# Two further blocks per turn in the graph layers' selection loop

## The reference, cut to what matters

```
def _rgcn_conv(x, W, Wroot, b, src, dst, etype):
    xs = x[src]
    seg = dst * R + etype
    sums = jax.ops.segment_sum(xs, seg, num_segments=N * R)
    cnt = jax.ops.segment_sum(jnp.ones_like(xs[:, 0]), seg, num_segments=N * R)
    mean = sums / jnp.maximum(cnt, 1.0)[:, None]
    return x @ Wroot + b + jnp.einsum('nrd,rde->ne', mean, W)
...
h = relu(_rgcn_conv(layernorm(x), W1, ...));  x = x + _rgcn_conv(h, W2, ...)
```

## Time and profile before

| what | value |
|---|---|
| median of 3 runs | 2932.53 us (2931.82 to 2933.41) |
| profiled execution, span of its instructions | 3487.9 us |
| the two graph layers in it | about 111 to 2657 us |
| indirect gathers of both layers | 1584 x 964 ns on POOL |
| PE | busy 71% of the span, mean granted clock 0.836 |

### The profile page before, as it was taken

One profiled execution on the slowest core, in us unless ns is written; L12 is line 12 of the kernel. 1 busy time (PEld: TensorE's weight loads), 2 busy tenths in 40 slices (PEclk: granted clock), 3 DMA queues, 4 the chain that ended last, 5 costly groups with the idle time before them and its releaser, 6 DMA issues.

```text
span 3487.9 us, 82172 instructions
## 1 busy us (share of the span) xinstructions
PE 2472.0 (71%) x19212; PEld 1832.7 (53%) x19213; DVE 1780.8 (51%) x4984; ACT 1225.2 (35%) x2344; POOL 1862.5 (53%) x1980
## 2 busy tenths in 40 slices
PE   1346787678687786346776587687877428999999
PEld 0113565356365564114564365465656327888887
DVE  7324455345355454124454354354545338787777
ACT  5202343134243342012343143152432126555554
POOL 1666566655655554666556656655563543333333
PEclk9557999589799898557998798798997559999999
DMA  6223323233332232223333333333335234322222
GB/s 216 80 83 112 88 87 91 85 87 89 87 88 87 86 89 64 86 84 97 98 104 97 94 100 99 94 105 95 101 100 163 102 115 132 96 73 71 71 70 59
DMA packets 165489, 333.24 MB, mean 96 GB/s; under 512 B 36078, under 2 KB 102346, under 8 KB 165288
## 3 DMA queue, kind: packets, MB, share of 16 engines
q0 software_dynamic: 91632, 247.48, 24.1%
q1 hardware_dynamic: 39912, 41.03, 4.0%
q10 hardware_dynamic: 33872, 43.92, 3.9%
HBM read 285.39 MB, written 49.07 MB: 96 GB/s over the span
## 4 chain that ended last, share of the span: by engine, by line
PE 44%; issue 22%; DVE 10%; another core or an unknown queue 9%; DVEq 7%; SPq 2%; ACT 2%; DMA 1%; ACTq 0%; POOLq 0%; POOL 0%
PE more_banks L1408 13%; PE sum_banks L1384 9%; PE sum_banks L1385 7%; PE more_banks L1535 4%; PE sum_banks L1535 3%; PE more_banks L1400 3%; PE sum_banks L1545 3%; DVEq L1044 3%; DVEq L1041 2%; DVE sels L1044 2%; DVEq L1027 1%; DVE stage L1079 1%; DVE sels L1036 1%; PE sum_banks L1426 1%
## 5 line engine op out<-in xcount | busy, mean ns | idle before, releaser
L509 POOL DMA_INDIRECT ring<-table,tabs x1584 | 1526.9, 964 | 1046.4 <-SPq L399 670.0
L1384 PE MATMUL sum_banks<-ring,sels 128*128 x2348 | 726.6, 311 | 630.1 <-issue 420.1
L1408 PE MATMUL more_banks<-weights,stage 128*128 128x256 f16 x5292 | 919.1, 290 | 22.0 <-issue 21.4
L1385 PE MATMUL sum_banks<-ring,sels 128*128 x2348 | 732.2, 313 | 41.5 <-issue 38.7
L1384 PEld LDWEIGHTS sum_banks<-ring,sels 128*128 128x128 f16 (+1 forms) x2348 | 242.4, 103 | 928.2 <-issue 896.9
L683 ACT ACTIVATE stage<-sum_banks,inv 128x256 f16<-128x256 f32 x784 | 328.1, 473 | 789.5 <-issue 384.9
L1408 PEld LDWEIGHTS more_banks<-weights,stage 128*128 128x128 f16 x5292 | 531.1, 104 | 135.3 <-issue 37.1
L1036 DVE SCALAR_TENSOR_TENSOR sels<-lane,win_off,tabs 128x256 f16<-128x256 f16 x792 | 349.4, 482 | 422.1 <-remote 181.9
L654 ACT ACTIVATE stage<-more_banks 128x1024 f16<-128x1024 f16 x392 | 402.0, 1026 | 419.1 <-remote 405.6
L1044 DVE TENSOR_SCALAR sels<-lane,win_off,tabs 128x128 f16 x780 | 260.6, 334 | 495.8 <-issue 339.6
L1079 DVE SCALAR_TENSOR_TENSOR stage<-sum_banks,inv,stage 128x256 f16<-128x256 f32 x784 | 347.0, 479 | 57.2 <-issue 40.2
(11 more groups left out here) (319 smaller groups left out, 2407.5 us busy)
## 6 DMA issues: line engine op xcount, KB each, us to landing
ring<-table,tabs POOLq DMA_INDIRECT x1584
weights<-L_ffn_W ACTq DMA_DIRECT2D x96, 178.5 KB
stage<-L_ffn_W ACTq DMA_DIRECT2D x16, 1024.0 KB, 5.0
edge_work<-lot_in SPq DMA_DIRECT2D x54, 260.0 KB
table<-edge_work ACTq DMA_DIRECT2D x49, 128.0 KB
lot_in<-sels SPq DMA_DIRECT2D x8, 260.0 KB
weights<-L_gnn_W SPq DMA_DIRECT2D x2, 1024.0 KB, 8.3
weights<-L_gnn_W ACTq DMA_DIRECT2D x2, 1024.0 KB
```

What stands on the lines that cost most here:

```text
L509: pool.indirect_dma_start(ring_rows[:, b % RING, 0:2 * D], None, tables[layer], bass.IndirectOffsetOnAxis(row_tab[:, b:b + 1], 0)).then_in ...
L1384: pe.matmul(to[:, 0:D + 1], hot, ring_row[:, ds(at + D, D + 1)], start=first, stop=last, skip_group_check=True)
L1385: return pe.matmul(to[:, 0:D], hot, ring_row[:, ds(at, D)], start=False, stop=last, skip_group_check=True)
L1408: return [pe.matmul(ps_out[par], rows[:, xp * KD + k, :], w16[:, wp, k, r * D:(r + 1) * D], start=part == PART_ORDER[0] and n == 0, stop=p ...
```

## The change

`more_blocks` takes two blocks per turn: one `scalar_tensor_tensor` over 128x256 makes both selections, after a wait for the second of the two blocks (also where the span ends on the first, and the second belongs to the next window). It signals `more_ready` once per turn. `more_sums` on PE steps by two: one wait, the first block's `add_rows`, and under a condition the second block's. `sel_more` gets a seventeenth slot, since the second of two starts at slot 15; a constant matrix moves to another place to make room.

```diff
-        sel_more = sels[:, 4 * P:4 * P + RING * P // 2].bitcast(f16).rearrange("p (s n) -> p s n", s=RING)
+        sel_more = sels[:, 4 * P:4 * P + (RING + 1) * P // 2].bitcast(f16).rearrange("p (s n) -> p s n", s=RING + 1)
...
             def more_blocks(layer, need, end, w):
                 with v.If(end > need):
-                    with v.Fori(need & MASK, end) as i:
-                        v.wait_ge(rows_ready[layer], i + 1)
+                    with v.Fori(need & MASK, end, 2) as i:
+                        v.wait_ge(rows_ready[layer], i + 2)
                         block = i.with_bounds(min_val=0, max_val=GATHERS - 1)
-                        v.tensor_scalar(flat(sel_more[:, ds(block & (RING - 1), 1), :]), lane16[:], win_off[:, ds(w, 1)], key_tab[:, ds(block, 1)],
-                                        ALU.add, ALU.is_equal).then_inc(more_ready[layer], 1)
+                        v.scalar_tensor_tensor(sel_more[:, ds(block & (RING - 1), 2), :], lane16[:].unsqueeze(1).to_broadcast([P, 2, P]), win_off[:, ds(w, 1)],
+                                               key_tab[:, ds(block, 2)].unsqueeze(2).to_broadcast([P, 2, P]), ALU.add, ALU.is_equal).then_inc(more_ready[layer], 1)
...
                 def more_sums(to, block, end):
                     with pe.If(end > block):
-                        with pe.Fori(block, end) as i:
+                        with pe.Fori(block, end, 2) as i:
                             pe.wait_ge(more_ready[layer], since)
                             slot = i & (RING - 1)
                             at = (slot * PITCH).with_bounds(min_val=0, max_val=(RING - 1) * PITCH)
                             add_rows(to, flat(sel_more[:, ds(slot, 1), :]), at, False, True).then_inc(steps_done[layer], 1)
                             pe.reg_add(since, since, 1)
+                            with pe.If(end > i + 1):
+                                at = (((i + 1) & (RING - 1)) * PITCH).with_bounds(min_val=0, max_val=(RING - 1) * PITCH)
+                                add_rows(to, flat(sel_more[:, ds(slot + 1, 1), :]), at, False, True).then_inc(steps_done[layer], 1)
```

More of the change, by code:

```diff
@@ L114, in build_program @@
         ring_rows = ring[:, :].bitcast(f16).rearrange("p (s c) -> p s c", s=RING)
-        sels = sb("sels", [P, 2 * BLOCKS])
+        sels = sb("sels", [P, 4 * P + (RING + 1) * P // 2])
         sel_flat = sels[:, 0:4 * P]
         sel = sel_flat.bitcast(f16).rearrange("p (s h b n) -> p s h b n", s=2, h=2, b=2)
-        sel_more = sels[:, 4 * P:4 * P + RING * P // 2].bitcast(f16).rearrange("p (s n) -> p s n", s=RING)
+        sel_more = sels[:, 4 * P:4 * P + (RING + 1) * P // 2].bitcast(f16).rearrange("p (s n) -> p s n", s=RING + 1)
         tabs = sb("tabs", [P, 3 * GATHERS + 4])
@@ L132, in build_program @@
         ident16 = sb("ident16", [P, P], f16)
-        ones16 = sb("ones16", [P, P], f16)
         lane16 = sb("lane16", [P, P], f16)
@@ L176, in build_program @@
         before16 = weights[:, 4280:4344].bitcast(f16)
+        ones16 = weights[:, 4400:4464].bitcast(f16)
         look_no = sels[:, 0:LOOKS]
@@ L464, in _ @@
             pool.memset(ident[:], 0.0).then_inc(pool_step, 1)
-            pool.memset(ones16[:], 1.0).then_inc(consts, 1)
+            pool.memset(ones16, 1.0).then_inc(consts, 1)
             small = dict(allow_small_or_imprecise_dtypes=True)
```

## The result

The changed kernel takes 2995.9 us in the median (2993.6 to 2998.0 in 4 runs) against 2932.4 for the kernel before beside it: a ratio of 1.021, with a 95% interval from 1.020 to 1.022, or 63 us more. The forecast was 2980, that is 48 more.

What follows compares the result with a forecast made beforehand. PE was taken to bound tiles 13 to 48, with gathers and PE's loop nearly level in tiles 0 to 12. 55 us lost less 7 saved made 48 on 2932.5, so 2980 us; own range 2950 to 3010, 8 in 10 2905 to 3015.

Steps and rivals of the forecast that it cites:

- PE's sequencer at the odd ends of the light tiles: Tiles 13 to 48, both layers: 182 windows ending on an odd block lose 65.5 us as recorded, 55 scaled.
- In tiles 13 to 48 PE sets the pace: Claim that PE's matmuls and sequencer bind these tiles, with gathers ahead and POOL waiting for free slots; chance 0.55.
- The rival that the gathers bind everywhere: Gathers, 1584 at 1.17 us, fill 93% of both layers, so nothing moves: 2930 to 2938 us; chance 0.15.
- The pairs: Rival: in tiles 0 to 12, 242 pairs give 48 us scaled while singles stay hidden: 2884 us; chance 0.20.
- A single's price: PE's sequencer gets 0.27 + 0.09 = 0.36 us more per window leaving the loop on an odd block.
- The scaling to 0.30: Recorded sequencer durations counted at about 1/1.19 in timed runs, from 2932.5 / 3487.9.
- nothing covers it: Claim that a single's 0.36 us is fully exposed, because PE has run dry when the loop is left.
- VectorE's 0.17 per single: A single block's selection turn takes 0.83 instead of 0.66 us; left out of the sum, upper end 96.
- The wait for one block more: Rival: in tiles 0 to 12 VectorE's longer wait costs at most 133 us; half gives 3045; chance 0.06.
- A full pair's 0.24: Each full pair in PE's loop, 121 per layer, saves 0.24 us of sequencer time.
- half of 14: Tiles 0 to 12: pairs less singles save 14 us scaled if PE binds, 0 if gathers do; 7 taken.
- PE's longer program: Rival: PE's program, 28% longer, no longer stays in instruction memory and is refetched: 3030 us and up; chance 0.04.

Runs made afterwards that it cites:

- jump: Kernel before plus a never-holding condition, hence one more taken branch, behind each of PE's 390 entered loops: 2974.7 us, ratio 1.014.
- base: Kernel before, unchanged, profiled a second time: 2932.4 us, span 2930.3.
- pe_half: Kernel before with only PE's loop taking two blocks per turn; VectorE still selects one block at a time: 2977.4 us, ratio 1.015.
- wait_only: Kernel before with VectorE waiting for one block more before each further selection: 2934.0 us, ratio 1.0007.
- dve_dose: Kernel before with VectorE writing one unread column per turn of its loop, PE unchanged: 2989.0 us, ratio 1.019.
- after_further_first: Changed kernel with VectorE making further selections ahead of the second of the first ones: 2984.2 us, ratio 1.018 against the kernel before.
- further_first: Kernel before with VectorE making further selections ahead of the second of the first ones: 2930.2 us, ratio 0.9991.
- not_taken: Kernel before plus an always-holding condition, with one register move as body, behind each of PE's 390 entered loops: 2960.1 us, ratio 1.009.
- pool_dose: Kernel before with POOL writing a padding column ahead of each of 1584 gathers, on its own semaphore: 2934.2 us, ratio 1.0001.

## Why the prediction came out as it did

The direction and the main step, PE's sequencer at the odd ends of the light tiles, were right. The size was 15 us short, and the picture behind it was wrong in one place.

*What bounds the kernel.* "In tiles 13 to 48 PE sets the pace" does not hold for the kernel before. POOL's 69.8 us of waiting belong to the execution with hold-ups; undisturbed, POOL gathers without a break there. The reading was also 0.305 us too large for each of the 59 waits: without that a gather takes (259.8 - 51.8) / 162 = 1.28 us and not 1.17, and 1584 of them fill all of the two layers' 1991 us and not 93%. The rival that the gathers bind everywhere had the right premise and the wrong conclusion. PE and VectorE keep up with the gathers by so little that 0.63 to 0.73 of what PE's sequencer gets on top in the light tiles comes out as time, in both layers nearly alike. Layer 2 takes some of it up in its heavy tiles: in tiles 1 and 2 the couples need 102.5 us before and 93.3 after. The pairs are not the reason, since `jump`, which has none, needs 90.9 there; I take it that PE arrives later and waits less for gathers. Why layer 1's heavy tiles take nothing up was not tested.

*A single's price* was right as recorded, 0.36 us. From the loop's last weight load to the product's it is 0.237 us before and 0.602 after (medians of some 270 windows in each trace). Weight loads of one such window, before:

```profile
404.03 0.10 PEld L1385 LDWEIGHTS sum_banks<-ring,sels 128*128 x1
404.28 0.22 PEld L1408 LDWEIGHTS more_banks<-weights,stage 128*128 128x128 f16 x3 [0.15 <-issue]
```

and after:

```profile
406.67 0.10 PEld L1385 LDWEIGHTS sum_banks<-ring,sels 128*128 x1
407.27 0.22 PEld L1411 LDWEIGHTS more_banks<-weights,stage 128*128 128x128 f16 x3 [0.51 <-issue]
```

The scaling to 0.30 was wrong by `base`. Two errors partly cancel, which is luck: the light tiles' 65.5 us unscaled, of which 48.0 come out (`pe_half`), stood in the sum as 55. And "nothing covers it" was too strong by what does not come out.

*VectorE's 0.17 per single*, left out of the sum and kept as its upper end, is where the missing term belongs, since VectorE's half of the change costs what is left: the change less `pe_half` is some 20 us by the medians and by the profiles, 12.8 in the light tiles and 7.7 in the heavy ones. The wait for one block more costs nothing beside PE's old loop (`wait_only`) and was not run beside the new one. A longer turn of VectorE alone costs 7 us in layer 1 (`dve_dose`); an earlier selection gives back 12 in the changed kernel and none before (`after_further_first`, `further_first`). I take it that VectorE's delay counts where PE's longer loop has made the couple late already; the wider instruction was not run beside PE's new loop without the pairing, so that these 20 us have this cause stays argued.

*A full pair's 0.24* exists and buys nothing. In tile 0 the changed loop starts its turns like this (weight loads):

```profile
175.77 0.10 PEld L1384 LDWEIGHTS sum_banks<-ring,sels 128*128 x1 [1.51 <-issue]
...
176.52 0.10 PEld L1384 LDWEIGHTS sum_banks<-ring,sels 128*128 x1 [0.52 <-issue]
...
178.29 0.10 PEld L1384 LDWEIGHTS sum_banks<-ring,sels 128*128 x1 [1.54 <-issue]
...
179.03 0.10 PEld L1384 LDWEIGHTS sum_banks<-ring,sels 128*128 x1 [0.52 <-issue]
```

The second block follows the first in 0.75 us where a turn took 1.07, and then PE stands 1.5 us until the next two: 2.5 us for two blocks, twice a gather's 1.25, and not the 1.9 that were foreseen. The "half of 14" in the heavy tiles was -7; `pe_half` shows -4.2, the whole change +3.5. That -4.2 is no gain of the pairs either: it is 9.0 more in layer 1 and 13.2 less in layer 2, where `jump` without pairs has 9.7 less. That is why the pairs, the reason one might expect a gain, could not win: they shorten PE exactly where PE waits for gathers.

*The other two rivals.* The wait for one block more costs nothing by itself (`wait_only`), and PE's longer program is not fetched again: 29 packets on q8 for 26, 12% more where its rows grow by 28%.

## What to carry to other kernels

Take a second profile when the span and the median disagree: hold-ups of one execution can make one engine look like the bound where another is. Unrolling a loop with run-time bounds pays per full turn and costs per odd end, so count both, and count each in the stages where that engine and not a transfer is late; here the full turns lay where gathers set the pace, the odd ends where there was hardly any slack. An engine's sequencer can be late while its array has work queued; here a different order of that engine's work gained next to nothing, and what remains to try is fewer or cheaper branches.

## What the runs showed of the hardware

- In `base` a jump of PE's sequencer takes 207 to 223 ns (0.267 us to the next instruction's start), a branch not taken 67 to 83 (in `not_taken` 0.126 us to the next instruction's start). The Trainium skill, page "Advanced Engine Details and Errata", section on control flow timing, gives about 108 ns for a compare-and-branch. The traces differ from it both ways.
- In `dve_dose` 32 instructions more in VectorE's loop over two tiles (two in each of its 16 loops) cost far more than their own time, in layer 2 alone, where the loop is then fetched again (158 packets for 47), while PE's program grew by 640 rows with no such effect (29 packets for 26).
- POOL leaves 0.305 us between two gathers (222.4 / 730 in layer 2 of `base`), and a write of 0.12 us fits in there for nothing (`pool_dose`).
